# One core, a fused transformer chain: waits on several semaphores written in another order

## The chip, the cores and the metric

One core of a Trainium2 chip runs the whole program in one launch. The metric is the device time in microseconds (us), the median of the runs; lower is better.

## What is computed

The reference is a chain of six residual blocks over x (2 x 256 tokens of 256 features) and a context of 2 x 4096 rows:

```
x = x + L0_xattn(layernorm(x), ctx)      cross attention, one head of 256, over 4096 keys
x = x + L0_attn(layernorm(x))            linear attention, 64 heads of 4, cumulative sums
x = x + L0_ffn(layernorm(x))             3 cycles of a coupling net (below)
x = x + L1_xattn(layernorm(x), ctx)      cross attention over the same context
x = x + L1_attn(layernorm(x))            16 heads of rank 64
x = x + L1_ffn(layernorm(x))             4-head attention, then 8 experts with a top-1 router
```

The coupling net is the part that this text speaks of most. For each of three cycles:

```
h = gelu(out @ w1 + b1);  h = gelu(h @ w2 + b2);  h = gelu(h @ w3 + b3);  tf = sigmoid(h @ w4 + b4)
out = out + (0.1 + adaptive_range * (0.7 * gf + 0.3 * tf - 0.5) * 2.0) * twist(out)
```

gf is a second small net on the mean over the tokens, computed once per batch element.

## The kernel before, in words

Each of the five engines has one hand-written program; they meet in semaphores alone (`wait_ge(sem, n)` before an instruction, `.then_inc(sem, 1)` behind one). TensorE (PE) makes all products and transposes into eight PSUM banks. ScalarE (ACT) evaluates Exp, Gelu and Tanh and copies the high halves of split numbers; VectorE (DVE) makes maxima, the low halves and the updates of x; GpSimd (POOL) makes low halves of the context and reciprocal roots; SP issues most DMAs.

The two cross attentions go in steps: for each of four blocks of 128 queries and eight chunks of 512 keys, `scores` (L685) makes a score tile, ACT copies it out (L1237), DVE takes its maximum (L1735), ACT exponentiates it (L1222), PE turns it (`turn`, L699), ACT and DVE split it (L1230, L1749), and `values` (L714, L716) multiplies it by the context. The small blocks (linear attention, coupling net, projections) are generators that each engine's program advances by one step at places written out in tables (`SIDE_AT`, `BETWEEN`), so their steps stand between steps of an attention. The order of work on each engine is thus fixed by hand.

The coupling net (`feed_forward(b)`, b the batch element, i the cycle, n = 3b + i) runs on three engines in turn. PE: L609 (w1, two halves; semaphore `f_1` after each), L615 (global net), L620 (w2, `f_2`), L624, L627 (w3, `f_3`), L631, L636 (w4, `f_4`). ACT: L1175 (Gelu of w1, two halves, `f_h1`), L1179, L1182, L1185, L1188 (Gelu, `f_h3`), L1191 (`f_gs`), L1193, L1198 (Tanh), L1201. DVE: L1711 to L1713 (`f_x`). `a_cum` counts the cumulative sums of the linear attention that runs before. Gelu and Exp are in different activation tables: the program holds an ACT_TABLE_LOAD right before the ACTIVATE that needs the other table, and it has the ACTIVATE's line.

The last block, `experts` (from L980 on PE): L997 brings tokens to their experts' places (`m_S` says that a place matrix is ready, `m_dis0` and `m_dis1` that ACT and DVE have copied the result out), L1039 the first product of two experts, L1048 transposes, L1067 the second product (`m_hT`: the transposed and biased halves, by DVE at L2104), L1076 brings results back. ACT L1419 and DVE L2097 copy the two halves of a hidden tile.

Of the kernel before, what the change touches and what calls it, by code (L numbers as in the profile page):

```python
# [78 lines left out]
SLOTS = 6  # L79
# [141 lines left out]
def build(nc, x, ctx, consts, cols, w_x, w_a, w_ao, b_a, w_f1, w_f2, w_f3, w_f4, w_g1, w_g2, w_g3, w_y, w_yv, b_yv,  # L221
          w_l, w_vo, w_in, w_out, rows6, w_gate, w_e1, b_e1, w_e2, b_e2, consts6, out):
    with ExitStack() as stack:
# [178 lines left out]
        def _(sp):  # L402
# [9 lines left out]
            for g in range(NG):  # L412
                if slot_free(g):
                    sp.wait_ge(s("ctx_hi"), slot_free(g))
                    sp.wait_ge(s("ctx_lo"), slot_free(g))
                sp.dma_start(stage[slot_of(g)], ctx_tiles[g]).then_inc(s(loaded(g)[0]), 16)
                for t in range(PE_TURNS, NG - 2):
                    if TURN_AT[t - PE_TURNS] == g:
                        sp.wait_ge(s("ctx_hi"), t + 1)
                        sp.wait_ge(s("ctx_lo"), t + 1)  # L420
# [26 lines left out]
            def load_vo(q):  # L447

                if q >= 2:
                    sp.wait_ge(s("vo_hi"), 2 * q - 2)  # L450
                    sp.wait_ge(s("vo_lo"), 2 * q - 2)
                sp.dma_start(vo_stage[:, 2 * (q % 2):2 * (q % 2) + 2], w_vo[2 * q:2 * q + 2].rearrange("h (c p) n -> p h c n", p=P))\
                    .then_inc(s("x_in%d" % (q % 2)), 16)
# [34 lines left out]
            load_w1(7)  # L488
            sp.wait_ge(s("m_closed"), 2)
            sp.wait_ge(s("m_pool"), 5)  # L490
# [8 lines left out]
        def _(pe):  # L499
# [95 lines left out]
            def feed_forward(b):  # L595
# [7 lines left out]
                for i in range(CYCLES):  # L603
# [29 lines left out]
                    pe.wait_ge(s("f_h3"), n + 1)  # L633
                    if i == 0:
                        pe.wait_ge(s("f_gs"), 3 * b + 3)
                    pe.matmul(ps[:, 7, SEQ:2 * SEQ], wf4, h3[b], start=True, stop=True).then_inc(s("f_4"), 1)  # L636
# [9 lines left out]
            def prep(g):  # L646

                pe.wait_ge(s("ctx_hi"), g + 1)
                pe.wait_ge(s("ctx_lo"), g + 1)
# [330 lines left out]
            def experts():  # L980
# [21 lines left out]
                pe.wait_ge(s("m_y1_lo"), 1)  # L1002
                for n, t in enumerate((0, 2)):
                    pe.wait_ge(s("m_S"), n + 1)
                    for h in range(2):
                        dispatch(t, h, *FIRST_PAIR)
                        dispatch(t, h, *OTHERS)
# [18 lines left out]
                def hidden(g):  # L1026

                    if g < 2:
                        pe.wait_ge(s("m_dis0"), g + 1)
                        pe.wait_ge(s("m_dis1"), g + 1)  # L1030
# [20 lines left out]
                def down(g):  # L1051
# [8 lines left out]
                    for e in pair:  # L1060
                        pe.wait_ge(s("w2_in%d" % e), 16 * (1 + (e < SLOTS - 2) * DEEP // SLOTS))
                    for half in range(2):
                        pe.wait_ge(s("m_hT"), 2 * g + 1 + half)
                        for f in range(half * FC // 2, (half + 1) * FC // 2):
# [55 lines left out]
        def _(act):  # L1120
            def project(what, b):
# [7 lines left out]
                if (what, b) == ("y", 0):  # L1129
                    act.wait_ge(s("px_qt"), k)  # L1130
                    for e in range(DC):
                        act.wait_ge(s("px_q"), (DC + 1) * k + e + 1)
                        act.activation(qT_of(what, b)[:, e, :], ps[:, side_banks(what, b)[1 - e], 0:SEQ], ACT.Identity,
# [29 lines left out]
            def feed_forward(b):  # L1163
# [3 lines left out]
                for i in range(CYCLES):  # L1167
                    n = b * CYCLES + i
                    if n >= 1:
                        act.wait_ge(s("f_2"), n)  # L1170
                    if i == 0:
                        act.wait_ge(s("a_cum"), 6 * b + 6)
                    for m in range(2):
                        act.wait_ge(s("f_1"), 2 * n + (m + 1 if i else 2))
                        act.activation(h1[b][:, m, :], ps[:, 7, 0:SEQ] if m and i else ps[:, 2, m * SEQ:(m + 1) * SEQ], ACT.Gelu,  # L1175
# [22 lines left out]
                    act.activation(th[b], ps[:, 7, SEQ:2 * SEQ], ACT.Tanh, bias=b4h, scale=0.5).then_inc(s("f_th"), 1)  # L1198
                    act.wait_ge(s("f_cA"), b + 1)
                    act.wait_ge(s("f_th"), 2 * n + 1)  # L1200
# [167 lines left out]
            def last_part():  # L1368
# [58 lines left out]
                for t in (2, 3):  # L1427
                    act.activation(zs[:, t - 2, :], ps[:, 7, (t - 2) * D:(t - 1) * D], ACT.Identity, scale=gate[:, t:t + 1])\
                        .then_inc(s("m_scaled"), 1)
                act.wait_ge(s("m_rstd"), 3)  # L1430
                act.wait_ge(s("m_closed"), 1)
# [31 lines left out]
        def _(pool):  # L1463
# [27 lines left out]
            for g in range(1, NG):  # L1491
                if g == 1:
                    pool.wait_ge(s("ctx_lo"), 1)
                if g == 2:
                    layernorm("x", 1)
                    pool.wait_ge(s("xn"), 2)
                pool.wait_ge(s(loaded(g)[0]), loaded(g)[1])
                pool.wait_ge(s("ctx_hi"), g + 1)
# [21 lines left out]
            def biases(k, tiles):  # L1520

                w = [P, tiles.stop - tiles.start, D]
                pool.wait_ge(s("w6_in"), 16 * 13)
                pool.wait_ge(s("xn_turned"), NORM["m", k] + 1)
# [32 lines left out]
        def _(dve):  # L1557
# [46 lines left out]
            def project(what, b):  # L1604
# [8 lines left out]
                if (what, b) != ("y", 0):  # L1613
                    if k >= 1:
                        dve.wait_ge(s("px_qt"), k)
                    for e in range(DC):
                        dve.wait_ge(s("px_q"), (DC + 1) * k + e + 1)
                        dve.tensor_scalar(qT[:, e, :], ps[:, (b1, b0)[e], 0:SEQ], C("%s_bq%d" % (what, e)), None, ALU.add)\
                            .then_inc(s("qT"), 1)
                yield  # L1620
                dve.wait_ge(s("px_qt"), k + 1)
                dve.wait_ge(s("qt_hi"), k + 1)
# [434 lines left out]
            def experts():  # L2057
# [50 lines left out]
                def y_out(g):  # L2108
# [5 lines left out]
                    publish(dve.tensor_tensor(ys, ps[:, 4, 0:D], b2r[:, g, :], ALU.add), "m_ys")  # L2114
                    dve.wait_ge(s("m_y_hi"), g + 1)
                    dve.tensor_tensor(yy[:, g, 1], ys, yy[:, g, 0], ALU.subtract).then_inc(s("m_y"), 1)

                h_out(0)
                for g in (1, 3):
                    dve.wait_ge(s("m_ST_ps"), g + 1)  # L2120
                    dve.wait_ge(s("m_ST"), g)
# [43 lines left out]
            dve.wait_ge(s("wx_in"), 32)  # L2165
# [78 lines left out]
```

## Time and profile before

| what | us |
|---|---|
| median of 3 runs | 533.56 (533.13 to 534.59) |
| span of the profiled execution, first to last instruction | 530.9 |
| PE busy | 502.4 (95%) |
| DVE busy | 348.6 (66%) |
| ACT busy | 287.1 (54%) |
| POOL busy | 89.5 (17%) |

The profiled execution has no time of its own beside its span; the median is 2.7 us above that span (533.56 - 530.9), which lies around the first and the last instruction. "Busy" of PE counts a matmul from its start to a modelled end. The chain of work that ended last is PE for 76% of the span, DVE 15%, ACT 5%, and 3% is "issue": time in which the engine waited for nothing that the profile shows. The times in the rows below are us from the span's start.

### The profile page before, as it was taken

Reading aid. Unit: us, or ns where it says so; the run is one execution under the profiler, and the core shown is the slowest. Engines: PE = TensorE matmul, PEld = TensorE weight load, DVE = VectorE, ACT = ScalarE, POOL = GpSimd, SP = SyncE. Lnnn points to the kernel's source line nnn. Section 1 sums busy time; section 2 is a strip of 40 time slices with the busy share of each in tenths; the row PEclk is TensorE's granted clock in tenths of the full one; section 3 lists DMA queues with packets and bytes.
Section 4 is the critical chain, followed back from the end, with each engine's and each line's share of the span. In section 5 each row is a group of like instructions: output and inputs, shape, how many; then the busy total and the mean of one; then the engine's idle time right before and its main releaser. Section 6 shows DMA issues by size and latency. Waiting matters only on the chain.

```text
span 530.9 us, 9285 instructions
## 1 busy us (share of the span) xinstructions
PE 502.4 (95%) x3482; PEld 348.2 (66%) x3482; DVE 348.6 (66%) x846; ACT 287.1 (54%) x631; POOL 89.5 (17%) x75
## 2 busy tenths in 40 slices
PE   9999999898998999999999999899999999999993
PEld 7665655566655555657645778688888878775552
DVE  4654647965447974357466647888889888876235
ACT  3777942537743138596166935888975545222111
POOL 2864120300001000000000410133320212120002
PEclk9999999999899998999999999999999999999997
DMA  9997450000000100000330031022228301694001
GB/s 289 302 284 156 100 120 1 0 2 1 1 0 2 30 1 1 2 0 1 116 122 1 2 115 46 4 78 81 81 93 305 144 1 43 219 349 183 1 1 40
DMA packets 45212, 44.04 MB, mean 83 GB/s; under 512 B 18672, under 2 KB 41200, under 8 KB 45040
## 3 DMA queue, kind: packets, MB, share of 16 engines
q1 hardware_dynamic: 44736, 42.72, 26.2%
q10 hardware_dynamic: 432, 0.73, 0.5%
q8 instruction: 28, 0.46, 0.4%
q14 instruction: 16, 0.13, 0.1%
HBM read 38.73 MB, written 0.52 MB: 74 GB/s over the span
## 4 chain that ended last, share of the span: by engine, by line
PE 76%; DVE 15%; ACT 5%; issue 3%; POOL 0%; DVEq 0%; ACTq 0%
PE ps L685 13%; PE ps L714 10%; PE ps L840 6%; PE ps L824 6%; PE ps L699 6%; PE ps L716 5%; PE ps L1039 3%; PE ps L1067 3%; PE ps L746 2%; PE ps L809 2%; PE ps L609 2%; PE ps L504 2%; PE ps L797 2%; PE ps L657 1%; PE ps L620 1%
## 5 line engine op out<-in xcount | busy, mean ns | idle before, releaser
L685 PE MATMUL ps<-ctx_tr,qtl 128*128 128x512 f16 x384 | 91.7, 383 | 0.0
L1735 DVE TENSOR_REDUCE mx<-arena 128x1 f32<-128x512 f32 x64 | 43.3, 682 | 38.8 <-ACT arena L1237 38.1
L1237 ACT ACTIVATE arena<-ps 128x512 f32<-128x512 f32 x64 | 38.0, 596 | 55.9 <-PE ps L685 55.9
L685 PEld LDWEIGHTS ps<-ctx_tr,qtl 128*128 128x128 f16 x384 | 37.4, 99 | 39.4 <-issue 3.4
L714 PE MATMUL ps<-ctx_nat,pth 128*128 128x512 f16 x172 | 58.6, 379 | 0.0
L1222 ACT ACTIVATE arena<-arena,small 128x512 f32<-128x512 f32 x64 | 45.7, 714 | 3.9 <-DVE small L1744 3.8
L840 PE MATMUL ps<-arena,ctx_tr 128*128 128x256 f16 x384 | 47.2, 273 | 0.1
L716 PE MATMUL ps<-ctx_nat,ptl 128*128 128x256 f16 x172 | 46.9, 273 | 0.0
L1467 POOL TENSOR_TENSOR rstd<-mv,small 128x2 f32<-128x2 f32 x13 | 9.1, 702 | 218.2 <-DVE mv L1589 214.9
L1749 DVE TENSOR_TENSOR ptl<-ps,pth 128x512 f16<-128x512 f32 x43 | 29.6, 689 | 23.6 <-ACT pth L1230 23.4
L699 PE MATMUL ps<-const,arena 128*128 128x128 f32 x256 | 39.6, 278 | 4.3 <-ACT arena L1222 4.2
L699 PEld LDWEIGHTS ps<-const,arena 128*128 128x128 f32 x256 | 31.0, 143 | 14.8 <-ACT arena L1222 7.3
L840 PEld LDWEIGHTS ps<-arena,ctx_tr 128*128 128x128 f16 x384 | 37.5, 98 | 4.7 <-DVE ctx_tr L1920 0.4
L1301 ACT ACTIVATE ctx_tr<-ps,small 128x256 f32<-128x256 f32 x64 | 29.6, 471 | 5.8 <-DVE work L1842 5.6
L1308 ACT ACTIVATE pth<-ps 128x512 f16<-128x512 f32 x32 | 18.9, 592 | 25.1 <-PE ps L809 25.1
L1230 ACT ACTIVATE pth<-ps 128x512 f16<-128x512 f32 x43 | 25.4, 590 | 12.0 <-PE ps L699 12.0
L714 PE MATMUL ps<-ctx_nat,arena 128*128 128x512 f16 x84 | 29.2, 385 | 0.1
L714 PEld LDWEIGHTS ps<-ctx_nat,pth 128*128 128x128 f16 x172 | 17.0, 99 | 16.9 <-issue 1.7
L1518 POOL TENSOR_TENSOR arena<-work,arena 128x512 f16<-128x512 f32 x16 | 18.5, 1158 | 55.0 <-ACT arena L1282 55.0
L1855 DVE TENSOR_SCALAR ctx_tr<-ctx_tr,small 128x256 f32<-128x256 f32 x64 | 26.2, 451 | 1.1
L1842 DVE TENSOR_SCALAR_CACHE_REDUCE work<-ps 128x256 f16<-128x256 f32 x64 | 24.3, 418 | 3.9 <-PE ps L797 3.8
L1920 DVE TENSOR_TENSOR ctx_tr<-ps,ctx_tr 128x512 f16<-128x512 f32 x32 | 21.9, 684 | 6.2 <-ACT ctx_tr L1314 6.2
(353 smaller groups left out, 1034.6 us busy)
## 6 DMA issues: line engine op xcount, KB each, us to landing
ctx_nat<-in_w_e SPq DMA_DIRECT2D x8, 1024.0 KB, 10.6
ctx_tr<-in_w_e SPq DMA_DIRECT2D x6, 1024.0 KB, 11.1
work<-in_ctx SPq DMA_DIRECT2D x8, 512.0 KB, 6.4
ctx_tr<-in_ctx SPq DMA_DIRECT2D x8, 512.0 KB, 8.3
work<-in_w_vo SPq DMA_DIRECT2D x8, 512.0 KB, 3.9
ctx_nat<-in_w_l SPq DMA_DIRECT2D x4, 512.0 KB, 5.4
arena<-in_w_e SPq DMA_DIRECT2D x2, 1024.0 KB, 6.7
wts<-in_rows SPq DMA_DIRECT2D x1, 1024.0 KB, 7.3
```

The costliest lines, as they stand in the source:

```text
L685: mm = pe.matmul(ps[:, n % 2, :], qtl[:, qh, d, u * P:(u + 1) * P], CT[:, t0:t0 + KT, kh, d, :], start=(i == 0 and d == 0), stop=(i == 2 a ...
L699: mm = pe.transpose(ps[:, 4 + j % 2, i * P:(i + 1) * P], S[:, (j) % SRING, i * P:(i + 1) * P], ident)
L714: pe.matmul(ps[:, acc, :], PH[j % PRING][:, i * P:(i + 1) * P], CN[:, t].rearrange("p h d -> p (h d)"), start=(c == 0 and i == 0), stop=Fa ...
L716: mm = pe.matmul(ps[:, acc, 0:D], PL[j % PRING][:, i * P:(i + 1) * P], CN[:, t, 0, :], start=False, stop=(c == NCH - 1 and i == KT - 1), s ...
L824: mm = pe.matmul(ps[:, 4 + i % 2, d * SEQ:(d + 1) * SEQ], xl5[b][:, xh, u, d * P:(d + 1) * P], pt[:, i % 2, pu], start=(n == 0), stop=(n = ...
L840: mm = pe.matmul(ps[:, 6 + b, t * D:(t + 1) * D], oT5[:, i % 2, oh, c, p * P:(p + 1) * P], vo[:, h, vh, c, :], start=(i % H5 == 0 and p == ...
L1222: act.activation(S[:, j % SRING, :], S[:, j % SRING, :], ACT.Exp, bias=ebias[:, u:u + 1], scale=SCALES[L], accum_out=ls[:, u, c:c + 1]).th ...
L1237: act.activation(S[:, n % SRING, :], ps[:, n % 2, :], ACT.Copy).then_inc(s("score_copied"), 1)
L1301: act.activation(P5[:, i % 2, t, :], ps[:, i % 2, t * SEQ:(t + 1) * SEQ], ACT.Exp, bias=nb5[:, i % 2, t:t + 1], scale=1.0 / 16, accum_out= ...
L1735: dve.tensor_reduce(mx[:, u, c:c + 1], S[:, n % SRING, :], AX.X, ALU.max).then_inc(s("score_max"), 1)
L1749: dve.tensor_tensor(PL[j % PRING], ps[:, 4 + j % 2, :], PH[j % PRING], ALU.subtract).then_inc(s("pt_lo"), 1)
L1855: o = dve.tensor_scalar(P5[:, i % 2, t, :], P5[:, i % 2, t, :], l5[:, i % 2, t:t + 1], 1024.0, ALU.mult, ALU.mult)
```

## The change

In the places listed, `wait_ge` lines before one instruction change their order; two waits move into a loop, behind its first one; on DVE a wait for `wx_in` goes (PE's product before it has waited for the same loads), and in `y_out` the waits for `m_y_hi` and `m_ys` swap. All other instructions stay as and where they were. The parts that the text below speaks of:

```diff
@@ feed_forward on PE
-                    pe.wait_ge(s("f_h3"), n + 1)
                     if i == 0:
                         pe.wait_ge(s("f_gs"), 3 * b + 3)
+                    pe.wait_ge(s("f_h3"), n + 1)
                     pe.matmul(ps[:, 7, SEQ:2 * SEQ], wf4, h3[b], start=True, stop=True).then_inc(s("f_4"), 1)
@@ experts on PE
-                pe.wait_ge(s("m_y1_lo"), 1)
                 for n, t in enumerate((0, 2)):
                     pe.wait_ge(s("m_S"), n + 1)
+                    if n == 0:
+                        pe.wait_ge(s("m_y1_lo"), 1)
...
                     if g < 2:
+                        pe.wait_ge(s("m_dis1"), g + 1)
                         pe.wait_ge(s("m_dis0"), g + 1)
-                        pe.wait_ge(s("m_dis1"), g + 1)
...
-                    for e in pair:
-                        pe.wait_ge(s("w2_in%d" % e), 16 * (1 + (e < SLOTS - 2) * DEEP // SLOTS))
                     for half in range(2):
                         pe.wait_ge(s("m_hT"), 2 * g + 1 + half)
+                        if half == 0:
+                            for e in pair:
+                                pe.wait_ge(s("w2_in%d" % e), 16 * (1 + (e < SLOTS - 2) * DEEP // SLOTS))
@@ project on ACT
                 if (what, b) == ("y", 0):
-                    act.wait_ge(s("px_qt"), k)
                     for e in range(DC):
                         act.wait_ge(s("px_q"), (DC + 1) * k + e + 1)
+                        if e == 0:
+                            act.wait_ge(s("px_qt"), k)
@@ feed_forward on ACT
                     n = b * CYCLES + i
-                    if n >= 1:
-                        act.wait_ge(s("f_2"), n)
-                    if i == 0:
-                        act.wait_ge(s("a_cum"), 6 * b + 6)
                     for m in range(2):
                         act.wait_ge(s("f_1"), 2 * n + (m + 1 if i else 2))
+                        if m == 0 and n >= 1:
+                            act.wait_ge(s("f_2"), n)
+                        if m == 0 and i == 0:
+                            act.wait_ge(s("a_cum"), 6 * b + 6)
                         act.activation(h1[b][:, m, :], ps[:, 7, 0:SEQ] if m and i else ps[:, 2, m * SEQ:(m + 1) * SEQ], ACT.Gelu,
...
+                    act.wait_ge(s("f_th"), 2 * n + 1)
                     act.wait_ge(s("f_cA"), b + 1)
-                    act.wait_ge(s("f_th"), 2 * n + 1)
                     act.activation(cpl[b], th[b], ACT.Identity, bias=cA, scale=cB).then_inc(s("f_th"), 1)
@@ experts on DVE
+                    dve.wait_ge(s("m_h"), 2 * g + 1)
                     dve.wait_ge(s("m_h_ps"), g + 1)
-                    dve.wait_ge(s("m_h"), 2 * g + 1)
```

The same kind of swap is made on SP (before the loads of context chunks, their DMA transposes, the loads of VO and the first store), on PE in `prep` (`ctx_lo` before `ctx_hi`), on POOL before the low halves of the context and in `biases`, on ACT before the last scaling (`m_closed` before `m_rstd`), and on DVE in `project` (`px_q` before `px_qt`, `qt_hi` before `px_qt`) and before the copies of the place matrices (`m_ST` before `m_ST_ps`).

How the built program changes at two places. The first is ACT's program where the coupling net begins (b = 0, i = 0). L1175 of before is L1178 of the change; the rows before and behind are Exp and Gelu steps. Before:

```order
L1222 ACTIVATE arena,ls<-arena,small 128x512
L1230 ACTIVATE pth<-ps 128x512 [waits av,pt]
L1175 ACT_TABLE_LOAD [waits f_1]
L1175 ACTIVATE wts<-ps,col 128x256 [waits a_cum]
L1175 ACTIVATE wts<-ps,col 128x256 [waits f_1]
L1179 ACTIVATE small<-ps,col 128x1 [waits f_g]
L1182 ACTIVATE wts<-ps,col 128x256 [waits f_2]
```

And now:

```order
L1225 ACTIVATE arena,ls<-arena,small 128x512
L1233 ACTIVATE pth<-ps 128x512 [waits av,pt]
L1178 ACT_TABLE_LOAD [waits a_cum]
L1178 ACTIVATE wts<-ps,col 128x256 [waits f_1] x2
L1182 ACTIVATE small<-ps,col 128x1 [waits f_g]
L1185 ACTIVATE wts<-ps,col 128x256 [waits f_2]
```

The wait for `f_1` stood ahead of the table load and stands behind it now; the wait for `a_cum` went the other way. The three other loads with this line stand behind `f_1` (one of them behind `f_1,a_cum`) before, and behind `f_2` (that one behind `a_cum,f_2`) now.

The second place is PE's program at the last pair of experts (L1048 transposes, L1059 a bias, L1067 the second product; L1049, L1060 and L1069 now). Before:

```order
L1048 MATMUL ps<-const,work 128x128 [waits m_hT,m_h]
L1048 MATMUL ps<-const,work 128x128 x7
L1059 MATMUL ps<-wts,const 128x256 [waits m_y]
L1067 MATMUL ps<-arena 64x256 [waits m_hT,w2_in7,w2_in6]
L1067 MATMUL ps<-arena 64x256 x7
```

And now:

```order
L1049 MATMUL ps<-const,work 128x128 [waits m_hT,m_h]
L1049 MATMUL ps<-const,work 128x128 x7
L1060 MATMUL ps<-wts,const 128x256 [waits m_y]
L1069 MATMUL ps<-arena 64x256 [waits w2_in7,w2_in6,m_hT]
L1069 MATMUL ps<-arena 64x256 x7
```

`m_hT` moved from the waiting instruction onto the matmul; the loads' semaphores moved onto the waiting instruction.

## Rows read from the trace of the kernel before

**Rows 1.** Busy time, share of the span, instructions: page, part 1.

```profile
PE 502.4 (95%) x3482; PEld 348.2 (66%) x3482; DVE 348.6 (66%) x846; ACT 287.1 (54%) x631; POOL 89.5 (17%) x75
```

**Rows 2.** L1175 alone: its table loads (min/median/max ns), and who waited for it.

```profile
L1175 ACT ACT_TABLE_LOAD  x4: 1283/1283/1283, 129.3 to 212.8; - x4
  PE ps L620: 2.2, 3
```

**Rows 3.** Timeline, coupling net n = 0: start, us, instruction, idle before and releaser.

```profile
129.28 1.28 ACT L1175 ACT_TABLE_LOAD   x1 [1.83 <-PE ps L609]
130.58 0.84 ACT L1175 ACTIVATE wts<-ps,col 128x256 f32<-128x256 f32 x2
131.10 1.13 PE L620 MATMUL ps<-wts 128*128 128x256 f32 x4 [1.56 <-ACT wts L1175]
```

**Rows 4.** The chain that ended last, same stretch: start, us, what.

```profile
129.24 0.02 ACTq L1174
...
130.57 0.01 issue
130.58 0.48 ACT wts L1175
131.06 0.04 issue
...
132.80 1.02 PE ps L627 x2
```

**Rows 5.** Timeline, n = 1.

```profile
145.81 1.28 ACT L1175 ACT_TABLE_LOAD   x1 [0.96 <-PE ps L609]
...
147.63 1.13 PE L620 MATMUL ps<-wts 128*128 128x256 f32 x4 [0.39 <-ACT wts L1175]
```

**Rows 6.** Timeline, n = 3.

```profile
198.56 1.28 ACT L1175 ACT_TABLE_LOAD   x1 [2.68 <-PE ps L609]
...
200.39 1.13 PE L620 MATMUL ps<-work,wts 128*128 128x256 f32 x4 [0.27 <-ACT work L1175]
```

**Rows 7.** Timeline, n = 4: the load begins as the ACTIVATE before ends.

```profile
212.06 0.60 ACT L1230 ACTIVATE pth<-ps 128x512 f16<-128x512 f32 x1
212.81 1.28 ACT L1175 ACT_TABLE_LOAD   x1
```

**Rows 8.** Timeline of ACT: two neighbours with a single wait, two with two waits.

```profile
134.38 0.26 ACT L1191 ACTIVATE small<-ps,small 128x1 f32<-128x1 f32 x1
134.67 0.39 ACT L1193 ACTIVATE small<-small 128x1 f32<-128x1 f32 x1
...
141.27 0.47 ACT L1198 ACTIVATE wts<-ps,small 128x256 f32<-128x256 f32 x1
...
141.83 0.60 ACT L1201 ACTIVATE wts<-wts,small 128x256 f32<-128x256 f32 x1
```

**Rows 9.** The chain that ended last, at L636 (n = 3) and at the last L1067.

```profile
202.08 0.66 PE ps L627 x2
...
203.39 0.14 issue
203.53 0.67 PE ps L636 x2
...
515.54 0.70 DVE arena L2104
516.25 0.14 issue
516.38 0.65 PE ps L1067 x4
```

**Rows 10.** Timeline at the first L1039.

```profile
482.95 0.29 DVE L2089 COPY ctx_tr<-ps 128x128 f32<-128x128 f32 x1 [0.40 <-PE ps L997]
...
483.43 3.65 PE L1039 MATMUL ps<-ctx_nat,ctx_tr 128*64 128x512 f32 x16
```

**Rows 11.** Four stretches: length, busy of each engine, then PE's granted clock.

```profile
129.50:132.90 3.40, 1.48 (x8) 0.95 (x8) 0.00 (x0) 2.67 (x6) 0.00 (x0) 1.00 0.00 0
132.90:136.30 3.40, 3.40 (x12) 2.02 (x13) 0.46 (x1) 2.34 (x4) 0.00 (x0) 0.50 0.00 0
201.20:204.60 3.40, 2.55 (x13) 1.21 (x12) 1.22 (x4) 2.54 (x7) 0.00 (x0) 1.00 0.01 2
204.60:208.00 3.40, 3.40 (x12) 1.72 (x11) 0.69 (x1) 2.85 (x7) 0.00 (x0) 0.50 0.00 0
```

**Rows 12.** Timeline of PE: first attention steps after n = 0, in and behind the slow stretch.

```profile
134.27 0.61 PE L714 MATMUL ps<-ctx_nat,arena 128*128 128x512 f16 x1
...
136.37 0.38 PE L714 MATMUL ps<-ctx_nat,pth 128*128 128x512 f16 x1
```

More of the change, by code:

```diff
@@ L413, in _ @@
                 if slot_free(g):
+                    sp.wait_ge(s("ctx_lo"), slot_free(g))
                     sp.wait_ge(s("ctx_hi"), slot_free(g))
-                    sp.wait_ge(s("ctx_lo"), slot_free(g))
                 sp.dma_start(stage[slot_of(g)], ctx_tiles[g]).then_inc(s(loaded(g)[0]), 16)
@@ L418, in _ @@
                     if TURN_AT[t - PE_TURNS] == g:
+                        sp.wait_ge(s("ctx_lo"), t + 1)
                         sp.wait_ge(s("ctx_hi"), t + 1)
-                        sp.wait_ge(s("ctx_lo"), t + 1)
                         turn_ctx(t)
@@ L449, in load_vo @@
                 if q >= 2:
+                    sp.wait_ge(s("vo_lo"), 2 * q - 2)
                     sp.wait_ge(s("vo_hi"), 2 * q - 2)
-                    sp.wait_ge(s("vo_lo"), 2 * q - 2)
                 sp.dma_start(vo_stage[:, 2 * (q % 2):2 * (q % 2) + 2], w_vo[2 * q:2 * q + 2].rearrange("h (c p) n -> p h c n", p=P))\
@@ L488, in _ @@
             load_w1(7)
+            sp.wait_ge(s("m_pool"), 5)
             sp.wait_ge(s("m_closed"), 2)
-            sp.wait_ge(s("m_pool"), 5)
             sp.dma_start(out_tiles[:, 0:2], X[:, 0:2, :]).then_inc(s("stored"), 16)
@@ L646, in prep @@
             def prep(g):
+                pe.wait_ge(s("ctx_lo"), g + 1)
                 pe.wait_ge(s("ctx_hi"), g + 1)
-                pe.wait_ge(s("ctx_lo"), g + 1)
                 if g >= 2:
@@ L1429, in last_part @@
                         .then_inc(s("m_scaled"), 1)
+                act.wait_ge(s("m_closed"), 1)
                 act.wait_ge(s("m_rstd"), 3)
-                act.wait_ge(s("m_closed"), 1)
                 act.activation(x0[:, 1, :], x0[:, 1, :], ACT.Identity, scale=rstd4[:, 1:2]).then_inc(s("m_scaled"), 1)
@@ L1496, in _ @@
                     pool.wait_ge(s("xn"), 2)
+                pool.wait_ge(s("ctx_hi"), g + 1)
                 pool.wait_ge(s(loaded(g)[0]), loaded(g)[1])
-                pool.wait_ge(s("ctx_hi"), g + 1)
                 pool.tensor_tensor(CN[:, g * KT:(g + 1) * KT, 1, :], stage[slot_of(g)], CN[:, g * KT:(g + 1) * KT, 0, :],
@@ L1522, in biases @@
                 w = [P, tiles.stop - tiles.start, D]
+                pool.wait_ge(s("xn_turned"), NORM["m", k] + 1)
                 pool.wait_ge(s("w6_in"), 16 * 13)
-                pool.wait_ge(s("xn_turned"), NORM["m", k] + 1)
                 pool.tensor_tensor(x0[:, tiles, :], x0[:, tiles, :], b6o.unsqueeze(1).broadcast_to(w), ALU.add).then_inc(s("x_bo"), 1)
@@ L1613, in project @@
                 if (what, b) != ("y", 0):
-                    if k >= 1:
-                        dve.wait_ge(s("px_qt"), k)
                     for e in range(DC):
                         dve.wait_ge(s("px_q"), (DC + 1) * k + e + 1)
+                        if e == 0 and k >= 1:
+                            dve.wait_ge(s("px_qt"), k)
                         dve.tensor_scalar(qT[:, e, :], ps[:, (b1, b0)[e], 0:SEQ], C("%s_bq%d" % (what, e)), None, ALU.add)\
@@ L1620, in project @@
                 yield
+                dve.wait_ge(s("qt_hi"), k + 1)
                 dve.wait_ge(s("px_qt"), k + 1)
-                dve.wait_ge(s("qt_hi"), k + 1)
                 dve.tensor_tensor(qtl[:, 1, :, b * SEQ:(b + 1) * SEQ], bank(b2, a=DC), qtl[:, 0, :, b * SEQ:(b + 1) * SEQ],
@@ L2113, in y_out @@
                     dve.wait_ge(s("m_y_ps"), g + 1)
-                    publish(dve.tensor_tensor(ys, ps[:, 4, 0:D], b2r[:, g, :], ALU.add), "m_ys")
+                    dve.tensor_tensor(ys, ps[:, 4, 0:D], b2r[:, g, :], ALU.add).then_inc(s("m_ys"), 1)
                     dve.wait_ge(s("m_y_hi"), g + 1)
+                    dve.wait_ge(s("m_ys"), g + 1)
                     dve.tensor_tensor(yy[:, g, 1], ys, yy[:, g, 0], ALU.subtract).then_inc(s("m_y"), 1)
@@ L2119, in experts @@
                 for g in (1, 3):
+                    dve.wait_ge(s("m_ST"), g)
                     dve.wait_ge(s("m_ST_ps"), g + 1)
-                    dve.wait_ge(s("m_ST"), g)
                     dve.tensor_copy(ST[:, g, :].bitcast(U32), turned_places(g).bitcast(U32)).then_inc(s("m_ST"), 1)
@@ L2164, in _ @@
             cut_lo(0)
-            dve.wait_ge(s("wx_in"), 32)
             next(first)
```

## The prediction

> **What bounds the kernel now.** I read the page first: PE is busy for 502.4 of 530.9 us [rows 1], so only some 28 us are open to a change that moves no work, and a wait matters where PE itself stands still or where a chain sets the end. Next came the view of who waited for whom, then the timeline at each place that the change touches, to see whether PE idles there. Most do not qualify. At `prep`, at the context's low halves on POOL, at SP's loads and transposes and at VO, the list of PE's waits has no entry for the waiting instruction's product; the swaps in `project` lie beside PE's own work or, in the stretch between the two attentions, beside DVE's linear attention, which sets what comes next there. Three kinds of place are left: the head of the coupling net (L1175), a few handoffs in front of PE, and what PE's clock makes of the first.
>
> **Part 1: the table load leaves the shadow of its wait.** The program's order shows more than a swap at L1175. The wait for `f_1` stands ahead of the Gelu table load before, and behind it now. The trace fits: at n = 0 ACT is idle for 1.83 us, the waiting instruction (ACTq) ends at 129.24, only then the load of 1.28 us runs, and the ACTIVATE starts at 130.58 [rows 3, 4]. `a_cum` and `f_2`, which stand ahead of the load now, were satisfied long before: the linear attention and the cycle before are over. So the load should begin when the ACTIVATE before it ends. There are four such loads, each 1283 ns [rows 2].
> - n = 0: ACT's idle 1.83 us holds the whole load. The ACTIVATE starts some 0.03 us behind `f_1`'s release, near 129.25 and not at 130.58: 1.33 us earlier. PE stands still for 1.56 us in front of L620 [rows 3], so all 1.33 go to PE, 0.23 stay. From L620 to the next Exp load, PE and ACT take turns, so both keep it. **1.33.**
> - n = 1: the idle is 0.96 [rows 5], so the ACTIVATE comes 0.93 earlier; PE has attention work there and idles 0.39. **0.39**; the rest is covered by L714 and L716.
> - n = 3: the idle is 2.68, the load fits; PE's idle is 0.27 [rows 6]. **0.27**; L685 covers the rest.
> - n = 4: ACT is busy until 212.66 and the load starts at 212.81 [rows 7]; at most 0.15 earlier, and PE does not wait at L620. **0.**
>
> Together 1.99 us. PE's idle on L1175 is 2.2 us in three times [rows 2], which is this sum and the rest of 0.23. Bounds: 0 if the load does not move, 2.2 as that row has it.
>
> **Part 2: the handoff.** Where an instruction's own wait ends last, it starts 0.03 to 0.04 us behind its releaser: L1193 at 134.67 after 134.64, L620 after an "issue" of 0.04 [rows 8, 4]. Where the waiting instruction ahead of it ends last, it takes longer: on ACT 0.09 (141.74 to 141.83) [rows 8], on PE 0.14 at L636 and at the last L1067 [rows 9], and 0.19 at the first L1039 (483.24 to 483.43) [rows 10]. The change puts the late wait on the instruction. PE gains 0.10 at L636 for n = 3, 0.10 at the last L1067 and 0.15 at the first L1039, all with PE idle and a chain behind them. **0.35.** L1201 and L2097 (0.06 each) and the other places are taken as 0: PE has attention or expert products then, or the end is set by DVE's last steps, whose waits are single. If that cover were gone they would add 0.06 a piece, about 0.5 over the chain of the coupling net. For L997 I take 0: it starts right behind the fill work, and PE waits later for ACT L1379 anyway.
>
> **Part 3: PE's clock.** In 129.5 to 132.9 PE is busy for 1.48 of 3.40 us, and behind it, in 132.9 to 136.3, the granted clock is 0.50, that is 1.2 and not 2.4 GHz [rows 11]. With Part 1 the idle of 1.56 in that stretch shrinks to 0.23 and attention work follows 1.33 earlier, so the reason for the fall should be gone. Its price: L627 takes 1.02 us there against 0.66 at full clock [rows 4, 9], 0.36 on the chain; then PE works without a pause from 134.27 to 136.37 [rows 12] at half speed, 2.10 us for 1.05 us of work. **1.4** together. The bounds are 0 (the fall stays) and 1.7 (half of 3.4). I take 1.4 because both pieces lie on PE's own path and ACT has idle time behind them to follow. A second fall is at 204.6 to 208.0, behind 3.4 us with PE busy 2.55 [rows 11]. There the change removes only 0.37 us of idle, so I leave it in the sum.
>
> **The sum.** 1.99 + 0.35 + 1.4 = 3.7 us from a span of 530.9, so 527.2. The median shown lies 2.7 above that span (its runs are 533.13 to 534.59, and a clock fall more or less would explain their spread). Taken from the median: 533.56 - 3.7 = **529.8**. A measurement of this kernel tells about 0.3% from no change, which is 1.6 us: faster means below 531.96.
>
> **The rivals.**
> 1. *The clock falls as before.* The coupling net's chain stays thin after L620: PE is then still waiting in turns with ACT, and the stretch at 201.2 fell with 2.55 of 3.40 busy. Then parts 1 and 2 alone: 533.56 - 2.34 = 531.2. Chance 0.20.
> 2. *The second fall goes too*, since its stretch gets 0.37 denser: some 1.4 more, 528.4. Chance 0.10.
> 3. *The change doesn't do what it says.* The load is not started before the ACTIVATE's own wait is satisfied, or a later stall gives the gain back (DVE is continuously busy in parts of 160 to 192, and PE waits for it). Then only Part 2 is left: 533.2. Against it: ACTq's own row ends before the load begins, so it was the waiting instruction that held it [rows 4]. Chance 0.09.
> 4. *The switch of tables costs twice what the load shows.* A switch would take twice the 1.28 us of the row, with a part of it unseen ahead of or behind the load. Begun at 127.45, where ACT falls idle, it would end at 130.0, and n = 0 gains 0.6; n = 1 nothing; n = 3 its 0.27. With Part 2 that is 1.2, and the clock falls as before: 532.3. Against it: the ACTIVATE starts 0.02 us behind the load's end, "issue" 0.01 [rows 3, 4]. Chance 0.03. The Trainium skill (ScalarE: Activation LUTs, "What ACT_TABLE_LOAD costs") gives about 1283 ns for the load and about 1380 ns for a drain. The trace agrees with the first and shows nothing of the second.
> 5. *Slower: the clock falls at new places.* The falls hang on how thin PE's work is at a given moment, and all that follows 129 moves by over 2 us. The router in front of the experts (464 to 478) is a string of small products with short waits. Each new fall costs at most 1.7 us by the price above. The gain of 2.34 with the old falls kept is used up from the second new one on: 533.56 - 2.34 + 3.4 = 534.6. For it: two falls are in the profile already. Against it: none is granted there now, and the work there stays as dense as it was. Chance 0.03.
>
> A swap that guessed wrong in some passes of a loop (the wait made early there is the late one) costs 0.06 to 0.15 a piece by Part 2 and can't turn the sign.
>
> **How the numbers follow.** The forecast has 0.55, the rivals 0.20, 0.10, 0.09, 0.03 and 0.03. The predicted time is the forecast's, 529.8. Its own spread is about 1 us either way, for a clock fall more or less in a run and the uncovered handoffs. The range runs from 528.0 (below rival 2) to 532.0 (above rival 1, at the edge of "same") and leaves out rivals 3 to 5 and the tails: about 0.18. Faster: 0.55 + 0.10 + most of the 0.20 = 0.83. Same: rivals 3 and 4 and the upper end of rival 1, 0.14. Slower: rival 5, 0.03.
>
> **What the profile of the changed kernel would show.** At n = 0 the table load starts near 127.5, right behind ACT L1233's end, and not behind L609; the ACTIVATE starts near 129.25 and PE's idle before L620 is about 0.2. At n = 1 the load starts near 144.9 (less what came before). PE's summed wait on L1178 falls from 2.2 to below 0.4. The "issue" of 0.14 before the last L1069 becomes 0.04. The granted clock stays at 1.00 behind n = 0. The prediction is wrong if the load still begins behind L609's end, if PE's idle before L620 only turns into one before L627 or L699, or if the clock reads 0.50 at more places than two.

## The result, and the profile after

| kernel | median us | range | runs |
|---|---|---|---|
| before | 533.35 | 532.83 to 535.03 | 6 |
| changed | 528.44 | 527.53 to 529.56 | 6 |

The ratio is 0.9916 (95% interval 0.9889 to 0.9942): 4.9 us faster, with 3.7 predicted. The changed kernel ran seven times more beside later experiments. Over all 13 runs its median is 528.99, and that of the 72 runs of the kernel before beside the experiments is 533.08, so the better estimate of the gain is 4.1 us. The profiled execution of the changed kernel took 529.56 us with a span of 527.8: 1.8 us lie around the span, and not the 2.7 that the prediction took.

Page of the changed kernel, part 1: PE has 2.8 us less busy time than in [rows 1], with no work taken away. A matmul at half clock takes longer (L714 0.61 us against 0.38 in [rows 12]).

```profile
PE 499.6 (95%) x3482; PEld 346.7 (66%) x3482; DVE 348.6 (66%) x846; ACT 287.2 (54%) x631; POOL 89.6 (17%) x75
```

The line of the coupling net's head (L1178 now, L1175 before) in the changed kernel: table loads, and who waited for it. It answers to [rows 2].

```profile
L1178 ACT ACT_TABLE_LOAD  x4: 1283/1283/1283, 127.7 to 208.0; - x4
...
  PE ps L620: 0.2, 1
```

The load takes the same 1283 ns, but PE's wait for this line is 0.2 us in one place where it was 2.2 in three.

The timeline of the changed kernel at n = 0, 1 and 3, beside [rows 3, 5, 6]:

```profile
127.72 1.28 ACT L1178 ACT_TABLE_LOAD   x1
129.48 0.84 ACT L1178 ACTIVATE wts<-ps,col 128x256 f32<-128x256 f32 x2 [0.48 <-PE ps L609]
...
142.18 1.28 ACT L1178 ACT_TABLE_LOAD   x1
143.48 0.94 ACT L1178 ACTIVATE wts<-ps,col 128x256 f32<-128x256 f32 x2
...
144.40 1.03 PE L620 MATMUL ps<-wts 128*128 128x256 f32 x4
...
195.12 0.84 ACT L1178 ACTIVATE work<-ps,col 128x256 f32<-128x256 f32 x2 [1.32 <-PE ps L609]
...
196.57 1.03 PE L620 MATMUL ps<-work,wts 128*128 128x256 f32 x4
```

At n = 0 the load now runs while PE works on L609, and ACT has 0.48 us of idle left between the load and the ACTIVATE. At n = 1 the load still ends last, but has moved up, and L620 has no idle before it. At n = 3 ACT waits for L609 with the table in place.

The chain that ended last in the changed kernel at n = 0, beside [rows 4]: neither the load nor ACTq is in it now, and L627, which took 1.02 us there, is a product at full clock (0.65 us, at 131.70 in this trace's timeline).

```profile
129.46 0.02 issue
129.48 0.48 ACT wts L1178
129.97 0.04 issue
130.01 1.14 PE ps L620 x4
```

The granted clock in the same four stretches as [rows 11], and in two in front of the experts:

```profile
129.50:132.90 3.40, 2.82 (x15) 1.73 (x15) 0.04 (x1) 2.10 (x7) 0.00 (x0) 1.00 0.00 0
132.90:136.30 3.40, 3.40 (x23) 2.18 (x22) 1.13 (x3) 3.34 (x7) 0.00 (x0) 1.00 0.00 0
201.20:204.60 3.40, 2.95 (x18) 1.74 (x17) 1.38 (x2) 3.37 (x9) 0.00 (x0) 1.00 0.00 0
204.60:208.00 3.40, 3.23 (x19) 2.02 (x17) 3.23 (x6) 3.40 (x9) 0.00 (x0) 1.00 0.00 0
464.80:468.20 3.40, 3.19 (x24) 2.65 (x22) 2.70 (x10) 0.69 (x4) 0.03 (x1) 1.00 1.10 348
468.20:471.60 3.40, 3.35 (x8) 2.69 (x9) 0.61 (x2) 0.33 (x1) 0.00 (x0) 0.50 1.10 348
```

Both falls of the trace before are gone and one has come at 468, in the stretch that rival 5 named. The difference between the starts of the same PE instruction in the two traces (after minus before) is a running account:

| up to | difference, us | step |
|---|---|---|
| n = 0, before L620 | +0.24 | start of the two executions |
| behind the stretch to 136.3 | -2.68 | load 1.33, clock 1.59 |
| behind n = 1 | -3.33 | 0.65 |
| behind n = 2 | -3.39 | L1201's handoff, 0.06 |
| n = 3, behind L620 | -3.92 | load 0.53 (0.42 at L620's start, 0.10 inside it) |
| n = 3, behind L636 | -3.99 | L636's handoff, 0.07 |
| 210 to 468 | -4.64 | the second fall is gone, 0.65 |
| behind the new fall | -2.99 | it costs 1.63 |
| end | -3.14 | handoffs behind L2097 and at the last L1069 |

So the trace holds both signs of the clock: two falls fewer (1.59 and 0.65), one more (1.63). Of the 2.2 us that the clock gave back, 1.6 were lost again at 468.

### The profile page after: what moved, and what is told of

Its sections match the earlier page's. It is cut to its first block, busy times and chain, and to the rows that moved or that the text cites. A ratio compares the mean times of both kernels' runs of the same rounds, so it can differ in the third digit from the quotient of the medians.

```text
span 527.8 us, 9284 instructions
## 1 busy us (share of the span) xinstructions
PE 499.6 (95%) x3482; PEld 346.7 (66%) x3482; DVE 348.6 (66%) x846; ACT 287.2 (54%) x631; POOL 89.6 (17%) x75
## 4 chain that ended last, share of the span: by engine, by line
PE 75%; DVE 15%; ACT 5%; issue 2%; DMA 1%; POOL 0%; DVEq 0%; ACTq 0%; POOLq 0%
PE ps L685 12%; PE ps L714 10%; PE ps L840 6%; PE ps L824 6%; PE ps L699 6%; PE ps L716 5%; PE ps L1040 3%; PE ps L1069 3%; PE ps L746 2%; PE ps L809 2%; PE ps L609 2%; PE ps L797 2%; PE ps L657 1%; ACT ctx_tr L1304 1%; PE ps L531 1%
## 5 line engine op out<-in xcount | busy, mean ns | idle before, releaser
L685 PE MATMUL ps<-ctx_tr,qtl 128*128 128x512 f16 x384 | 90.4, 379 | 0.0
L714 PE MATMUL ps<-ctx_nat,pth 128*128 128x512 f16 x172 | 58.6, 379 | 0.0
L716 PE MATMUL ps<-ctx_nat,ptl 128*128 128x256 f16 x172 | 46.9, 273 | 0.0
L714 PE MATMUL ps<-ctx_nat,arena 128*128 128x512 f16 x84 | 28.6, 379 | 0.1
L714 PEld LDWEIGHTS ps<-ctx_nat,pth 128*128 128x128 f16 x172 | 16.9, 98 | 16.9 <-issue 1.7
```

What stands on the lines that cost most here:

```text
L685: mm = pe.matmul(ps[:, n % 2, :], qtl[:, qh, d, u * P:(u + 1) * P], CT[:, t0:t0 + KT, kh, d, :], start=(i == 0 and d == 0), stop=(i == 2 a ...
L714: pe.matmul(ps[:, acc, :], PH[j % PRING][:, i * P:(i + 1) * P], CN[:, t].rearrange("p h d -> p (h d)"), start=(c == 0 and i == 0), stop=Fa ...
L716: mm = pe.matmul(ps[:, acc, 0:D], PL[j % PRING][:, i * P:(i + 1) * P], CN[:, t, 0, :], start=False, stop=(c == NCH - 1 and i == KT - 1), s ...
```

## The experiments

Two theories beside mine were set against it. **A**, mine: the gain is the table load that leaves the shadow of its wait, the clock falls that the late load brought, and a few tenths of handoffs. **B**: it is many handoffs, in some twenty places. **C**: the load is real, but the clock is chance. The kernels ran in three sets, each on one chip beside its own runs of the kernel before: 25 runs, median 534.29; 29 runs, median 533.11; 18 runs, median 532.74.

Each run also lists its mean granted clock, and this sorts them. The 72 runs of the kernel before:

| mean granted clock | runs | mean us | range |
|---|---|---|---|
| 0.994 to 0.995 | 14 | 530.41 | 530.15 to 530.79 |
| 0.991 | 7 | 531.15 | 530.80 to 531.48 |
| 0.988 to 0.990 | 21 | 532.95 | 532.50 to 533.53 |
| 0.985 to 0.986 | 30 | 534.69 | 533.35 to 535.32 |

The profiled executions say what the top group is: two kernels in which nothing at n = 0 was repaired (the second and the seventh below) had no fall before the closing microseconds, with spans of 528.1 and 528.5 and a mean clock of 0.995. So 530.4 is the kernel before without clock falls, and the rest of its spread, up to 4.9 us, goes with the clock. A median says how often the falls come; the top group says what the work and the waits cost. Both are read below. The expectations were written before this was seen.

**1. The head alone.** The kernel before with one of the change's edits, and **2. all but the head**, its complement.

```diff
-                    if n >= 1:
-                        act.wait_ge(s("f_2"), n)
-                    if i == 0:
-                        act.wait_ge(s("a_cum"), 6 * b + 6)
                     for m in range(2):
                         act.wait_ge(s("f_1"), 2 * n + (m + 1 if i else 2))
+                        if m == 0 and n >= 1:
+                            act.wait_ge(s("f_2"), n)
+                        if m == 0 and i == 0:
+                            act.wait_ge(s("a_cum"), 6 * b + 6)
```

> The kernel before with one edit of the change alone: at the head of ScalarE's part of the feed-forward the wait on f_1 is written first and the waits on f_2 and a_cum behind it. Theory A (the gain is the table load that no longer stands behind the last wait, and the clock falls that the later start brought): nearly all of the change's gain, 528.4 to 529.2 us, the load at n=0 at 127.5 to 128.0 us, PE waiting for L620 less than 0.4 us there, and no clock fall at 133. Theory B (the gain is many small handoffs in some twenty places): 533.0 us, 0.3 below the kernel before. Theory C (the fall's going is chance, unrelated to the load): 530.9, which is the load's 2.4 us alone, with a fall at 133 still there.

> The changed kernel with that one edit undone and every other kept. Theory A: 532.9 to 533.3 us, since the traces of before and after show only 0.2 to 0.3 us at the other places (0.07 at L1201, 0.05 at L636, 0.07 at the last L1067, 0.06 behind L2097), the load back at 129.3 to 129.5, and the clock at 0.50 near 133. Theory B: 528.8. Theory C: 532.9 or 531.5, by whether the fall at 133 is there.

Measured: the head alone 529.48 us (529.20 to 529.92, 7 runs), ratio 0.9928 (0.9896 to 0.9960). All but the head 534.25 (529.92 to 534.80, 12 runs), ratio 1.0001 (0.9976 to 1.0027). The one edit is the change, as far as these medians can tell; B falls. The first came out 0.3 above what I expected, because every one of its runs had a granted clock of 0.989 to 0.992; its profiled execution fell at 468.2. The second lies 1.0 above my 532.9 to 533.3, as the kernel before in its set does (534.29), and its profiled execution did not have the fall near 133 that I expected. The timeline of the head alone, PE and ACT at n = 0, shows the product at full clock:

```profile
127.20 1.28 ACT L1175 ACT_TABLE_LOAD   x1
128.96 0.84 ACT L1175 ACTIVATE wts<-ps,col 128x256 f32<-128x256 f32 x2 [0.48 <-PE ps L609]
...
129.49 1.13 PE L620 MATMUL ps<-wts 128*128 128x256 f32 x4 [0.23 <-ACT wts L1175]
...
131.19 0.65 PE L627 MATMUL ps<-wts 128*64 128x256 f32 x2 [0.36 <-ACT wts L1182]
```

**3. n = 0 alone**, and **4. all but n = 0**: the same edit under a condition (n > 0 in the fourth run).

```diff
+                    late = n == 0
+                    if not late and n >= 1:
...
+                        if m == 0 and late and n >= 1:
```

> The kernel before with the head's waits turned at n=0 only; n=1, 3 and 4 keep their order. Theory A: the load's 1.33 us at n=0 and the clock fall's 1.4 to 1.6 there go, so 530.2 to 530.8 us, with the n=1 and n=3 losses (0.65 and 0.4 in the shift between the traces) still there. Theory B: 533.2. Theory C: 532.0, the load alone.

> The complement of the run that turned the head's waits at n=0 only: here n=0 keeps its old order and n=1, 3 and 4 are turned. Theory A: the clock fall at 133 stays, and only the 0.65 and 0.4 us of n=1 and n=3 go (and with them perhaps the fall at 204): median 532.3 to 533.2, lowest runs without a fall 529.1 to 529.4. Theory B (no part of the head matters much by itself): 534. If the clock at n=0 is not what n=0's turn bought: both halves alike, about 531.5.

Measured: n = 0 alone 530.22 us (528.72 to 532.39, 12 runs), ratio 0.9932 (0.9908 to 0.9956); all but n = 0, 532.04 (530.31 to 533.53, 12 runs), ratio 0.9977 (0.9955 to 0.9998). The first is worth 4.1 us in its set, the second 1.1 in another. In the top group by clock, n = 0 alone has five runs, 528.72 to 529.13, mean 528.91: 1.5 below the 530.41 of before, where the load's 1.33 was forecast. No run of the fourth kernel had a clock above 0.992, so its time without a fall was not seen. Its trace, set against that of before like the changed one above, has the same two steps: 0.65 at n = 1 and 0.53 at n = 3. Its profiled execution had the load late (128.98, ACT idle 1.83), and yet no fall at 133, which I had expected to stay. Nor do all falls go with the third: one of its runs is at 532.39 with a clock of 0.986.

**5. The old order of waits, with the table fetched early.** One Gelu of a single column ahead of the waits pulls the load forward.

```diff
+                    if i < 2:
+                        act.activation(small[:, 60 + 2 * b + i:61 + 2 * b + i], C("gc_b1"), ACT.Gelu)
                     if n >= 1:
                         act.wait_ge(s("f_2"), n)
```

> The kernel before with every wait in its old order, and one Gelu of 128x1 (a column of the constants into an unused column of small) put in front of the head's waits at n=0, 1, 3 and 4. It pulls the table load ahead of all waits and costs one short ACTIVATE of 0.2 to 0.3 us each. Theory A: what counts is when the load runs and not how the waits are written, so 528.4 to 529.4 us, the load at n=0 at 127.5 to 127.8 as the first thing after L1230. Theory B: 533.3 or a little more for the four added operations. Theory C: as in the first run, 530.9.

Measured: 529.44 us (529.09 to 529.97, 7 runs), ratio 0.9922 (0.9892 to 0.9951), the same as the head alone in the same set (529.48). Timeline of ACT at n = 0:

```profile
127.04 1.28 ACT L1170 ACT_TABLE_LOAD   x1
128.34 0.20 ACT L1170 ACTIVATE small<-col 128x1 f32<-128x1 f32 x1
128.87 0.84 ACT L1177 ACTIVATE wts<-ps,col 128x256 f32<-128x256 f32 x2 [0.33 <-PE ps L609]
```

No wait changed its place here, so the order of the waits is only the means. What counts is that the table is there when `f_1` comes. The added ACTIVATE takes its 0.20 us out of ACT's idle time, which is 0.33 here and 0.48 above.

**6. The clock part alone.** The load stays late; PE gets 12 spare products in the time in which it waits.

```diff
                     yield
+                    if n == 0:
+                        keep_busy(12, 3)
                     for c in range(2):
                         pe.wait_ge(s("f_h1"), 2 * n + c + 1)
```

> The kernel before with its waits as they were, and 12 spare products of 128x256 (half precision, into bank 3 ahead of the product that overwrites it) on TensorE behind the gc product at n=0, in the 1.56 us that it spends waiting there. Only the clock part of the theory is touched: the load stays at 129.3 and L620 at 131.1. Theory A: the fall at 133 never comes, the others may, so the runs that have it now come down by 1.6 us, median 532.0 to 532.8 against 534.3; the lowest runs, which have no fall at all, stay at 530.2 to 530.5. If the fall at 133 had not come from TensorE's rest at n=0: 534.3, with a fall at 133.

Measured: 531.77 us (530.39 to 532.73, 12 runs) against 533.11 in its set, ratio 0.9979 (0.9954 to 1.0004). Not one of the 12 runs is in the group at 0.985 to 0.986, where the kernel before has 10 of 29 in this set, and the highest is 532.73. So 1.3 us come back without a wait or a load moved, and the falls have to do with PE's rest at n = 0. That rest does not decide alone: the profiled executions of the second, fourth and seventh kernels have it and no fall at 133. Windows of this kernel, with a fall further on:

```profile
129.50:132.90 3.40, 2.84 (x20) 1.96 (x19) 0.00 (x0) 2.68 (x6) 0.00 (x0) 1.00 0.00 0
132.90:136.30 3.40, 3.37 (x19) 1.93 (x20) 0.97 (x2) 2.74 (x6) 0.00 (x0) 1.00 0.02 5
...
471.60:475.00 3.40, 3.40 (x13) 2.95 (x12) 1.40 (x5) 0.00 (x0) 0.10 (x1) 0.50 1.11 350
```

The interval reaches just above 1, so the weight here lies on the groups and on the windows rather than on the ratio.

**7. Three handoffs alone**: the turned pairs at ScalarE's L1201, TensorE's L636 and TensorE's L1067, put into the kernel before. The first of them:

```diff
-                    act.wait_ge(s("f_cA"), b + 1)
                     act.wait_ge(s("f_th"), 2 * n + 1)
+                    act.wait_ge(s("f_cA"), b + 1)
```

> The kernel before with three of the change's other edits: the turned pairs at ScalarE's L1201, TensorE's L636 and TensorE's L1067. Theory A by the shift between the traces: 0.07 + 0.05 + 0.07 = 0.2 us, so the lowest runs (without a clock fall) at 530.1 against 530.3 and the median at 534.1; the last L1067 starts 0.04 us behind its releaser and not 0.14. Theory B: these three would carry a fifth of the change at the least, 533.2.

Measured: 531.84 us (530.05 to 534.90, 12 runs), ratio 0.9980 (0.9951 to 1.0008). This median is a count of clock falls and not a gain: six runs are at 530.05 to 530.54 and six at 533.14 to 534.90. The six of the top group have a mean of 530.27, 0.14 below the 14 runs of before, with 0.2 expected; the two ranges overlap, so the time alone doesn't prove it. The chain that ended last, in this kernel, shows the step itself, beside the 0.14 of [rows 9]:

```profile
513.26 0.70 DVE arena L2105
513.97 0.04 issue
514.01 3.67 PE ps L1068 x32
```

**8 to 11. The fall at 468.** The changed kernel with 14 spare products between the router's products, first into bank 2; then 14 and 8 of them into bank 7; and the changed kernel itself beside the latter two. In the first of these the spare products overwrite what bank 2 holds of z1 for tile 3 (I had written that nothing reads it there), so the output lacks that part; its times are within 0.5 us of those of the kernel that writes to bank 7.

```diff
+                keep_busy(5, 7)
                 pe.wait_ge(s("m_yT"), 2)
...
+                keep_busy(6, 7)
                 for b in range(B):
                     pe.wait_ge(s("m_o"), 2 + b)
```

The kernels with 14 have three more ahead of the z1 products; the one with 8 has 4 and 4 at the two places shown.

> The changed kernel with 14 spare products of 128x256 (3, 5 and 6, into bank 2, which nothing reads there) between the router's narrow products of last_attention, at 463 to 467 us. They cost 14 x 0.11 = 1.5 us if TensorE is the path there, as the trace shows it to be. What the fall at 468 costs is 1.6 us in the runs that have it (529.2 to 529.6), so it breaks even with those: 529.0 to 529.6, but with every run alike and no fall at 468. If the products lie in a wait: 527.6. If the fall has nothing to do with TensorE's narrow products: 530 to 531.2, the fall on top of the fillers.

> The changed kernel as it is, beside the next three on one chip. Runs without a clock fall at 527.4 to 527.9, runs with the fall at 468 at 529.2 to 529.6; median between these, ratio to before 0.990 to 0.992.

> The changed kernel with the same 14 spare products of 128x256 in the router's stretch as in the run before, now into bank 7, which the transposes behind them overwrite. Theory A (the fall at 468 comes of TensorE's narrow products): every run alike at 528.6 to 529.1 us, no fall before the end. If the rest before was only due to what bank 2 lost: falls at 468 again and 529 to 531.

> The same with 8 spare products (4 and 4). They cost 0.6 to 0.8 us: 528.2 to 528.5 in the runs without a fall. If 8 are enough, all runs lie there and this beats the changed kernel wherever that falls; if not, a part of them is at 529.8 to 530.2 with the fall. I expect the fall to stay in a part of the runs, median 528.5 to 529.5.

| kernel | median us | range | runs | ratio to before |
|---|---|---|---|---|
| changed, 14 spare into bank 2 | 528.95 | 528.54 to 529.07 | 6 | 0.9919 (0.9892 to 0.9946) |
| changed again | 529.28 | 527.95 to 529.55 | 7 | 0.9926 (0.9899 to 0.9954) |
| changed, 14 spare into bank 7 | 528.53 | 528.22 to 528.75 | 6 | 0.9919 (0.9892 to 0.9946) |
| changed, 8 spare into bank 7 | 527.97 | 527.83 to 528.17 | 6 | 0.9909 (0.9882 to 0.9935) |

With 14 the spread shrinks from 1.6 us to 0.5, and with 8 to 0.3; I had expected 8 not to be enough. The version with 8 has the lowest median of this study: its six runs are below six of the seven of the changed kernel beside it, and its median is 1.3 us lower. That is 0.25%, near what a measurement can tell, and the changed kernel's own lowest runs (527.53) are lower still; what it buys is that the fall doesn't come. Windows of the changed kernel run again, and of the one with 8:

```profile
464.40:467.80 3.40, 3.27 (x25) 2.91 (x24) 2.95 (x11) 0.40 (x3) 0.31 (x1) 0.99 1.10 348
467.80:471.20 3.40, 3.36 (x9) 2.52 (x8) 0.61 (x2) 0.67 (x2) 0.00 (x0) 0.50 1.10 348
```

```profile
464.80:468.20 3.40, 3.33 (x30) 2.96 (x29) 2.44 (x8) 0.51 (x3) 0.00 (x0) 1.00 1.10 348
468.20:471.60 3.40, 3.21 (x22) 2.95 (x23) 1.66 (x8) 0.41 (x2) 0.18 (x1) 1.00 1.10 348
```

The 8 cost little: 527.98 in the mean against 527.75 for the four runs of the changed kernel with a clock of 0.994 or more, so 0.2 us and not the 0.6 to 0.8 that I had counted; the 14 in bank 7 cost 0.8 by the same reckoning, and not 1.5. The timeline of the kernel with 8 has PE idle for 0.26 us before L973, waiting for ACT L1406, so PE is not the path throughout.

**12. The kernel before with the falls filled**: the load as late as it was, 12 spare products at n = 0, 4 at n = 3 and the 14 in the router.

> The kernel before, every wait in its old order and the table load as late as it was, with spare products where the clock fell: 12 at n=0, 4 at n=3 and the 14 in the router's stretch. Theory A: no fall, all runs alike at 531.4 to 531.9 us (530.3 of the runs of before without a fall, and 1.3 for the router's products), against 532 to 535 of most runs of before; and 2.6 to 2.8 above the changed kernel with the same 14, which is the load and the handoffs alone. If the clock is not ruled by what TensorE does there: a spread of 4 to 5 us as the kernel before has.

Measured: 531.41 us (531.27 to 531.85, 12 runs), with no fall in the profiled execution before the end. The spread of 4.3 us in the same set's runs of the kernel before (530.59 to 534.89) has become 0.6. Against the changed kernel with the same 14, also without a fall, it is 531.41 - 528.53 = 2.9 us: this is the price of the late loads and the handoffs, free of the clock. The shift between these two traces is 2.79 us, in the same steps as in the account above: 1.33 at n = 0, 0.65 at n = 1, 0.53 at n = 3, and the rest, 0.3, at four handoffs. Theory C fails by this run and the sixth, as far as the falls can be filled; what is left of it is that the same stretch is not followed by a fall each time. The load stands where it did (timeline of ACT):

```profile
129.04 1.28 ACT L1180 ACT_TABLE_LOAD   x1 [1.83 <-PE ps L609]
130.34 0.84 ACT L1180 ACTIVATE wts<-ps,col 128x256 f32<-128x256 f32 x2
```

## Why the prediction was right, and where its terms were off

| term | predicted | measured | from |
|---|---|---|---|
| load, n = 0 | 1.33 | 1.33 (1.5 in run 3) | shift of the traces, top group |
| load, n = 1 | 0.39 | 0.65 | shift |
| load, n = 3 | 0.27 | 0.53 | shift |
| load, n = 4 | 0 | 0 | shift |
| handoffs | 0.35 | 0.3 | shift |
| these together | 2.34 | 2.8 | shift; 2.66 by 530.41 - 527.75, 2.9 by run 12 |
| clock | 1.4 | 1.5 in the mean | see below |
| sum | 3.7 | 4.1 | medians of 72 and 13 runs |

**Part 1 was right in kind and too small at n = 1 and n = 3.** I counted only the idle ahead of L620 that the timeline lists, and the wait costs PE more than that. The chain that ended last has it. Before, n = 1:

```profile
147.10 0.48 ACT wts L1175
147.59 0.04 issue
147.63 1.13 PE ps L620 x4
```

Changed, n = 1:

```profile
144.45 0.11 PE ps L716
144.56 0.86 PE ps L620 x4
```

1.13 - 0.86 = 0.27, and 0.39 + 0.27 = 0.66 against 0.65 in the shift. The 0.27 has two parts. The listed idle begins at the modelled end of the product before; without a wait, L620 starts 0.16 us ahead of that end (144.40 where L716 runs from 144.29 to 144.56). And the first product behind an idle stretch takes 0.48 us and not 0.38, 0.10 more. The first single product of a group, before at L620 (n = 1) and L609 (n = 3), then changed at L620 (n = 1) with the product ahead of it:

```profile
147.63 0.48 PE L620 MATMUL ps<-wts 128*128 128x256 f32 x1 [0.39 <-ACT wts L1175]
196.47 0.48 PE L609 MATMUL ps<-work,wts 128*128 128x256 f32 x1 [0.78 <-DVE work L1602]
...
144.29 0.27 PE L716 MATMUL ps<-ctx_nat,ptl 128*128 128x256 f16 x1
144.40 0.38 PE L620 MATMUL ps<-wts 128*128 128x256 f32 x1
```

L609 has no second wait inside its group and shows the same 0.48, so this is not a wait for the second half that ACT delivers. At n = 3 the same two parts make 0.27 + 0.16 + 0.10 = 0.53, as measured. At n = 0 PE is idle before L620 in both kernels, so both parts stay, L620 is as long as before, and the gain is the 1.33 forecast.

**Part 2 was right at the last L1067 (0.09) and, less, at L636 (0.07); wrong at the first L1039.** L1201 and the handoff behind L2097, which I had put at 0, gave 0.06 and 0.07; that the sum of 0.3 lies near my 0.35 is thus luck in part. At the last L1069 the "issue" is 0.04 where it was 0.14:

```profile
512.49 0.70 DVE arena L2107
513.19 0.04 issue
513.24 3.67 PE ps L1069 x32
```

At the first L1040 I had read the gap of 0.19 between DVE's end and L1039's start in [rows 10] as a slow handoff of an idle PE. It is still 0.18 in the changed kernel:

```profile
479.97 0.29 DVE L2092 COPY ctx_tr<-ps 128x128 f32<-128x128 f32 x1 [0.39 <-PE ps L997]
...
480.44 1.08 PE L1040 MATMUL ps<-ctx_nat,ctx_tr 128*64 128x512 f32 x4
```

The chain that ended last goes from L997 straight into this product in both kernels (3.67 us of L997, then L1039 at 483.50 before; the same 3.67, then L1040 at 480.51 after), and neither has idle time of PE in front of the product. The step that failed is "all with PE idle", which I had not looked up for this place; the row shown was DVE's. With the late wait on the instruction itself the product still starts 0.18 behind DVE's end, and not 0.03 to 0.04; what holds it stays open.

**Part 3 was right that n = 0 rules the first fall, and its size was near.** The fall cost 1.59 us in the trace of before, with 1.4 forecast: 0.48 at L627 and L631, where I had 0.36 for L627 alone, and 1.10 behind them, where I had 1.05. But "the clock falls at 133" is no property of the kernel before: it came in some executions and not in others. So the term has to be read as a mean. Over the 72 runs the kernel before lies 533.01 - 530.41 = 2.6 us above its runs without a fall, and the changed kernel, over 13, 528.82 - 527.75 = 1.1. The difference is 1.5. Two things lie behind the 1.1 and the 2.6 that the forecast didn't have: the second fall is gone as well in the profiled execution (rival 2, which priced it at some 1.4; it cost 0.65), and a fall at 468 is often there (the place and the price of rival 5, 1.63 against 1.7 at most). The mechanism of rival 5 was thus real, and I held it too unlikely; that the 1.5 of the mean lies next to the 1.4 forecast is partly luck, as it is the balance of three falls. Rival 5 did not decide because one fall at 468 is less than the load and the falls at 133 and 204. Rival 3 fell with the trace, rival 4 too: the load was done 0.48 us before the ACTIVATE at n = 0. Rival 1 was wrong.

**The baseline was off by 0.9.** I took the distance between the median and the span, 2.7 us, as time around the span. It is 1.8 in every run here whose span is listed (532.9 with 531.1, 527.53 with 525.7). The profiled execution of before thus took 532.7 us, 0.9 below the median of the three runs. Its mean clock, 0.988, is that of the third group of the table above, in which the median of the 72 runs lies too. Taken from itself the same sum would have given 529.0.

## What to carry to other kernels

The load of a table in front of an ACTIVATE is held by a wait that stands ahead of it, and freed when that wait sits on the ACTIVATE; look for loads that begin just as a producer ends, and put the wait that comes last on the instruction, or touch the table early with one small operation. Ask of an idle engine not only how long it stands, but what its clock does behind it. A wait can cost more than the idle time listed (0.65 us against 0.39 here): compare the starts of the same instructions in two traces. Where the runs of a kernel spread by more than the change is worth, sort them by granted clock before comparing medians.

## What the runs showed of the hardware

- The same stretch is followed by a fall in one execution and not in another. All but the head had the same thin stretch as [rows 11] in its profiled execution, 1.48 of 3.40 us busy, and kept its clock. What decides it between executions stays open; nothing here was made to test it.

```profile
129.20:132.60 3.40, 1.48 (x8) 0.94 (x8) 0.00 (x0) 2.68 (x6) 0.00 (x0) 1.00 0.00 0
132.60:136.00 3.40, 3.40 (x19) 1.95 (x20) 0.97 (x2) 2.74 (x6) 0.00 (x0) 1.00 0.00 0
```

- PE was busy for 3.19 of 3.40 us ahead of the fall at 468 in the changed kernel, 2.0 of them with products of 8 columns (L955, L961), and the clock fell all the same. With 8 spare products of 256 columns there the profiled execution kept it, and the mean clock of all six runs was 0.994 to 0.996. So the busy share of a stretch did not tell this fall in advance. Its price was 1.63 us.
- The first product of an L609 or L620 group (128x256, f32) behind idle time took 0.48 us all ten times in the two traces, whether the idle was 0.10 us or 1.56; without idle before it, 0.38 at full clock.
- The Trainium skill (ScalarE: Activation LUTs, "What ACT_TABLE_LOAD costs") gives a drain of about 1380 ns beside the load of 1283. No run here shows the former: where the load ended last (n = 1), the ACTIVATE began at 143.48, 0.02 us behind the load's end, and n = 0 gained the load's whole 1.33.
